# Decoder block on one core: the value blocks of cross-attention, issued in pairs

## What is computed

```python
B, S, E = q.shape            # 4, 512, 512
H, KV = (NUM_Q_HEADS, NUM_KV_HEADS)      # 32, 8
D = E // H                   # 16
G = H // KV                  # 4
scale = math.sqrt(D)
qh = q.reshape(B, S, KV, G, D).transpose(0, 2, 3, 1, 4)
kh = k.reshape(B, S, KV, D).transpose(0, 2, 1, 3)
vh = v.reshape(B, S, KV, D).transpose(0, 2, 1, 3)
scores = jnp.einsum('bkgsd,bktd->bkgst', qh, kh) / scale
weights = jax.nn.softmax(scores, axis=-1)
out = jnp.einsum('bkgst,bktd->bkgsd', weights, vh)
...
x = x + _L0_attn_ref(_layernorm(x, axis=-1), L0_attn_weight_qkv, L0_attn_weight_proj)
x = x + _L0_xattn_ref(_layernorm(x, axis=-1), ctx_512, ctx_512)
x = x + _L0_ffn_ref(...)
```

## Time and profile before

| | us |
|---|---|
| median of 3 runs | 2031.02 |
| lowest and highest | 2029.3, 2034.8 |
| the profiled execution | 2037.13 |
| its span, first to last instruction | 2035.4 |

### The profile page before, as it was taken

How to read it: one execution, slowest core, us unless ns; L and a number is a source line. 1 busy time by engine, 2 the same in 40 slices (tenths; PEclk the granted TensorE clock), 3 DMA queues, 4 the chain that set the end, 5 groups by cost and what they waited for, 6 DMA issues and landing times. The chain is left out here.

```text
span 2035.4 us, 28770 instructions
## 1 busy us (share of the span) xinstructions
PE 1882.0 (92%) x9769; PEld 1330.5 (65%) x9769; DVE 1085.9 (53%) x2253; ACT 966.6 (47%) x1789; POOL 261.8 (13%) x751
## 2 busy tenths in 40 slices
PE   6999989998899989988999998998899999899998
PEld 4677667666677667665444443443388998788888
DVE  7433433342433433454677777778645236565656
ACT  3433433343433433333677776776632135565641
POOL 1000000000000000041143242432003200000015
PEclk9999999999899999998899998999969999999999
DMA  3000000000000000000000060000012237667656
GB/s 134 32 1 1 21 33 1 1 2 21 32 1 1 21 1 1 1 11 0 1 6 1 1 238 13 0 0 1 1 45 86 91 106 264 244 244 267 243 193 223
DMA packets 73393, 131.64 MB, mean 65 GB/s; under 512 B 4512, under 2 KB 35232, under 8 KB 73248
## 3 DMA queue, kind: packets, MB, share of 16 engines
q1 hardware_dynamic: 68128, 113.01, 15.7%
q0 software_dynamic: 5120, 16.78, 2.4%
HBM read 96.75 MB, written 33.03 MB: 64 GB/s over the span
## 5 line engine op out<-in xcount | busy, mean ns | idle before, releaser
L1504 DVE TENSOR_REDUCE xmax<-ps 128x1 f32<-128x512 f32 x512 | 329.0, 686 | 114.3 <-PE ps L1066 106.2
L1329 ACT ACTIVATE xp<-ps 128x1024 f32<-128x1024 f32 x256 | 262.9, 1029 | 140.7 <-PE ps L1077 136.8
L1262 ACT ACTIVATE probs<-ps,nmax 128x128 f32<-128x128 f32 (+3 forms) x256 | 135.4, 529 | 313.2 <-DVE nmax L1480 312.4
L1066 PE MATMUL ps<-k,q 64*128 64x512 f32 x496 | 219.2, 483 | 33.0 <-DVE xmax L1504 33.0
L1480 DVE TENSOR_REDUCE nmax<-ps 128x1 f32<-128x128 f32 (+3 forms) x256 | 125.4, 490 | 229.5 <-PE ps L908 223.5
L1066 PEld LDWEIGHTS ps<-k,q 64*128 64x128 f32 x496 | 86.6, 188 | 201.0 <-DVE xmax L1504 162.7
L908 PE MATMUL ps<-k_t,q_t 128*128 128x128 f32 (+3 forms) x512 | 201.0, 476 | 0.0
L1077 PE MATMUL ps<-q3m,k 64*128 64x512 f32 x512 | 183.8, 456 | 0.0
L987 PE MATMUL ps<-pt,v_s 128*128 128x128 f32 (+3 forms) x512 | 159.5, 457 | 22.7 <-ACT v_s L1311 20.9
L149 PE MATMUL ps<-ident,probs 128*128 128x128 f32 x704 | 128.8, 289 | 44.9 <-DVE probs L1488 29.2
L149 PEld LDWEIGHTS ps<-ident,probs 128*128 128x128 f32 x704 | 91.7, 147 | 100.2 <-issue 67.8
(11 more groups left out here) (179 smaller groups left out, 3403.7 us busy)
## 6 DMA issues: line engine op xcount, KB each, us to landing
w_raw<-in_w_t SPq DMA_DIRECT2D x56, 704.0 KB, 6.8
w_raw<-in_w_t SPq DMA_DIRECT2D x28, 768.0 KB, 5.7
rows_x<-w_raw SPq DMA_DIRECT2D x1, 9984.0 KB, 30.1
mixed<-rows_x SPq DMA_DIRECT2D x39, 256.0 KB, 7.3
rows_y<-y_s SPq DMA_DIRECT2D x39, 256.0 KB, 7.1
w_raw<-in_w_qkv_t SPq DMA_DIRECT2D x4, 1536.0 KB, 6.9
res<-in_x SPq DMA_DIRECT2D x4, 1024.0 KB, 12.2
w_raw<-in_w_proj_t SPq DMA_DIRECT2D x4, 1024.0 KB, 5.3
```

The lines of the kernel that those rows point to most:

```text
L1066: pe.matmul(ps[:, XS + op[1] % 2, :], q3[half_of(h), (kv + 1) % 2, h // 2, i * P:(i + 1) * P], k3[half_of(h), (kv + 1) % 4, :], start=True ...
L1262: act.activation(probs[:, u % 4, 0:w], ps[:, S_BANK + u % 2, 0:w], ACT.Exp, bias=nmax[:, u % 4:u % 4 + 1], accum_out=rsum[:, u % 4:u % 4 + ...
L1329: act.activation(xp[:, kv % 2, 2 * pair:2 * pair + 2, t, :], ps[:, XST + 2 * (t % 2):XST + 2 * (t % 2) + 2, :], ACT.Exp, scale=X_SCALE).th ...
L1504: dve.tensor_reduce(xmax[:, slot, i, h:h + 1], ps[:, bank + u % 2, :], AX_X, ALU.max, negate=True).then_inc(s_xmax, 1)
```

## The change

Only `cross_steps` is changed. In every round two scores are handed out, one ahead of the transposed score and one behind it, where it was three in even rounds and one in odd ones. Value blocks are issued in rounds 3 and 7, two at a time, where one was issued in each odd round.

```diff
     for k in range(8):
-        units = [("s", next(s_units)) for _ in range(1 if k % 2 else 3)] if m_left >= 1 else []
-        if k % 2 == 0:
-            ops += units[0:1]
-            units = units[1:]
+        units = [("s", next(s_units)) for _ in range(2)] if m_left >= 1 else []
+        ops += units[0:1]
         if m_left >= 0:
             ops.append(("st", k))
-        ops += units[0:1]
+        ops += units[1:]
         if k in turns and (m_left >= turns[k][2] if turns[k][0] != "o" else kv >= 2):
             ops.append(("t",) + turns[k])
-        ops += units[1:]
-        if kv >= 1 and m_left >= -1 and k % 2:
-            ops.append(("pv", k // 2))
+        if kv >= 1 and m_left >= -1 and k % 4 == 3:
+            ops += [("pv", k // 2 - 1), ("pv", k // 2)]
     return ops
```

## The result

The changed kernel takes 2076.9 us (median of 4 runs, 2072.0 to 2082.6) against 2030.6 us (median of 4 runs of the kernel before): a ratio of 1.0225 with a 95% interval of 1.0192 to 1.0258. The profiled execution took 2082.6 us with a span of 2080.8, 45.4 us more than the one of before. The sign and the range of the prediction hold, and its mechanism holds in most items; the 62 us of its sum were about 46.

The account below looks back on a forecast made before the run. PE's sequence was taken to bound an item's first half, DVE the place between scores 11 and 12. Terms 21.6 + 40.6 = 62.2 us made the profiled 2037.1 into 2099.3, less 6.1: 2093 us; forecast 2075 to 2110, range 2051 to 2110.

Parts of the forecast that it names:

- What bounds the item, and the gate: Cross-attention item: PE's sequence bounds the first half; score 12 waits for DVE's maximum of score 10, 1.49 us after, 0.49 before.
- First half: Joining value blocks 0 and 1 behind score 7 takes 2.43 us instead of 2.57, a gain of 0.14 us an item.
- Full clock: Cross-attention items grow by 0.71 us each, 30 times, plus 0.3 us in the last item: 21.6 us.
- The clock: Granted clock falls to 0.50 around scores 12 to 15 in nearly every item, 1.4 us each, 29 times: 40.6 us.
- the bound of 2.9: Upper bound in us on an item's clock cost, if the slow stretch runs on through the pair of value blocks.
- The sum: Cross-attention stage: the full-clock 21.6 us and the clock's 40.6 us add up to 62.2 us.
- Items that are longer now wait outside the blocks and pay too: Already longer cross-attention items, such as those building keys, were also to grow by 0.71 us at full clock.
- the count of 30 items: Of 32 cross-attention items, all but the first and last pay 0.71 us each at full clock: 21.3 us.
- (a): Rival: the clock holds or falls in few cross-attention items; 2053 us, up to 2073 if half fall; chance 0.15.
- (b): Rival: the slow stretch runs on through the pair in most items; 2140 us; chance of over 2110 us 0.05.
- (d): Rival: the blocks' place decides nothing, as another chain, such as GpSimd's maxima, sets the item's length; 2031 us; chance 0.03.
- (c): Rival: faster, if score 12 did not wait for score 10's maximum and both pairs gained 0.14 us; 2023 us; chance 0.02.

Follow-up runs that it names:

- e7: The changed kernel with DVE's division and addition of a finished result moved behind the maximum of score 11; ratio 1.0155 to the kernel before.
- e1: The kernel before with value block 2 alone moved to the item's end, beside block 3; ratio 1.0264 to the kernel before.
- e2: The kernel before with value blocks 0 and 1 alone joined behind score 7; ratio 1.0020 to the kernel before.
- e3: The changed kernel with the matmul of score 11 issued six times into the same bank instead of once; ratio 1.0077 to the kernel before.
- e5: The kernel before with blocks 0 and 1 joined behind score 7 and blocks 2 and 3 behind score 11; ratio 0.9947 to the kernel before.
- e8: The changed kernel with the matmul of score 11 issued three times instead of once; ratio 1.0210 to the kernel before.
- e4: The kernel before with the 10 MB zero fill started later, by one more wait on the SyncE queue; ratio 0.9979 to the kernel before.

## Why the prediction came out as it did

**What bounds the item, and the gate.** Right. Score 12 kept its place behind score 8 to 0.01 us and the stop grew by 1.00 us, the block that was taken away; e7 moved the gate by moving DVE's result, and e1 has the whole loss with block 2 alone.

**First half.** Right in size in regular items (-0.13 us in e2 against -0.14). Wrong in being a gain on its own: e2 as a whole is 0.2% slower.

**Full clock.** Right in a regular item: 0.71 worked out, 0.74 in e3. Too large as a term: 21.6 us were taken, and e3 shows 16 as a whole and 10.7 from the first copy to the last. Its 19 regular distances gave 13.8 there, the other twelve -3.1, where the sum had 8.

**The clock.** Right in kind, and nearly right in size for regular items: 1.4 us were taken, 17.26 - 15.82 = 1.4 are measured between the two traces. In five distances with copies 18.6 to 19.1 us apart (and in one of 20.0) the slow stretch ran on. That is the bound of 2.9. Four of them are regular, two regular ones had no fall (15.6 us), and together these six explain most of the 4 us by which the regular distances exceed their 40. As a term it was too large: 40.6 us were taken, and 30 to 33 are measured by e3. 24 of the 29 distances fell instead of nearly all, and five had a slow stretch before already, where the sum allowed for one. The argument was partly wrong, too. It put weight on the length of the stretch without value products; e5 has a longer one at 1.00. Stops of PE among its matmuls matter (e3 against e8 and the change, e7), but five items of the changed kernel and five of e8 passed the same stop, so what decides in one item stays open.

**The sum.** The step that failed is "Items that are longer now wait outside the blocks and pay too", and with it the count of 30 items (29 for the clock). Twelve distances were to give 22 us and gave -0.7. Where DVE makes moments the wait lies outside the blocks, but at the item's start, right behind the pair, so that the pair covers a part of them; five of the twelve had slow stretches before as well, two of them double ones; and one lost its 4.67 us stop because the loop's turn slid out from under the transfers. All three could have been read from the trace of before: the moments of the item at 1241.80 start on DVE at 1241.07, and PE finishes block 3 only at 1241.66; the slow stretches stand in its clock; and DVE is idle for 4.67 us from 1220.6 us.

**The rivals.** (a), the clock holds or falls in few items, is excluded by the trace, with 24 of 29 fallen; its time of 2053 is near e3's (2046 laid on 2031), where the clock was mostly made to hold. The guidance behind it (the Trainium skill, "TensorE: Matmul & The Clock Gate", Why this matters for your kernels) speaks of idle gaps longer than these; here stops of 0.8 to 1.5 us once an item were enough in most items. (b), the double stretch, came in 6 of the 29 distances and not in most. (d) is excluded by e1, where the place of block 2 alone costs 2.6%. (c) decided where it was said to decide: a pair that fits the stop gives a faster kernel, e5, but it is another order than this one.

**Open.** In e7, 14 distances between copies in a row are 17.06 to 17.08 us, each with one slow stretch, though its stops would allow an item near 15.3 us at full clock. Such a regular pattern was not foreseen. Why the item's length settles just there was not tried, and neither was why in the first batch of the changed kernel two items in turn add up to about twice as much (18.6 and 15.6) with a fall in the first only.

## What to carry to other kernels

When an in-order engine waits at one place of a loop, look at what has been put ahead of that wait: moving it away costs its whole length, moving more work there gains until the wait is full. A stop of TensorE in each turn of a loop, here 1.4 to 1.5 us, can cost more by the clock (30 us) than the longer item costs at full clock (at most 16 us); filling it, even with repeated matmuls, shows in one run which of the two it is. And an effect worked out for a loop's regular body shouldn't be multiplied by all its turns: list those with extra work, and ask of each what hides behind what.

## What was not expected of the hardware

A kernel that issues 5 matmuls more in each of some 30 items ran 1.5% faster. With a stop of 1.03 us the clock falls in most regular items, with one of 0.33 us in none, in otherwise equal items; yet the same stop of 1.38 us is passed at 1.00 in every second item of the first batch. And VectorE stood idle for 4.67 us at a loop's turn while DMA transfers ran on into it, with no semaphore in between; the profile lists that only as "issue". With the transfers moved away (e4) 1.96 us are left.
